# An eight-headed cross-attention rebuilt: context prepared two stages earlier, queries made per tile, scores over 64 inputs in float32, softmax turned in float32

## The reference, cut to what matters

```python
def _L1_xattn_ref(x, context, Wq, Wk, Wv, Wo, bo):      # H = 8, D = 64
    q = (x @ Wq).reshape(B, Nq, H, D)
    k = (context @ Wk).reshape(B, Nkv, H, D)
    v = (context @ Wv).reshape(B, Nkv, H, D)
    sim = jnp.einsum('bihd,bjhd->bhij', q, k) * SCALE   # D ** -0.5
    attn = jax.nn.softmax(sim, axis=-1)
    out = jnp.einsum('bhij,bjhd->bihd', attn, v).reshape(B, Nq, H * D)
    return out @ Wo + bo
...
x = x + L0_attn(layernorm(x));  x = x + L0_xattn(layernorm(x), ctx)   # one head of 256
x = x + L0_ffn(layernorm(x));   x = x + L1_attn(layernorm(x))
x = x + L1_xattn(layernorm(x), ctx);  x = x + L1_ffn(layernorm(x))    # signed weights
```

## Time and profile before

| | us |
|---|---|
| median of 3 runs | 1231.96 (1227.54 to 1237.32) |
| the profiled execution, its own time | 1229.34 |
| its span, first to last instruction | 1227.6 |
| mean granted TensorE clock | 0.894 |
| stage `cross_attention` L = 0 (preparation 283.2 to 334.3, loop to 415) | 132 |
| stage `cross_attention` L = 1, preparation (833.8 to 888.8) | 55.0 |
| stage `cross_attention` L = 1, loop and tail (888.8 to 1038.6) | 149.8 |
| stage `signed_ffn` (from 1039.5) | 188 |

### The profile page before, as it was taken

One profiled execution on the slowest core, in us unless ns is written; L12 is line 12 of the kernel. 1 busy time (PEld: TensorE's weight loads), 2 busy tenths in 40 slices (PEclk: granted clock), 3 DMA queues, 4 the chain that ended last, 5 costly groups with the idle time before them and its releaser, 6 DMA issues. The chain is left out here.

```text
span 1227.6 us, 21445 instructions
## 1 busy us (share of the span) xinstructions
PE 1001.8 (82%) x8092; PEld 580.7 (47%) x8092; DVE 848.9 (69%) x1735; ACT 654.3 (53%) x1106; POOL 337.1 (27%) x409
## 2 busy tenths in 40 slices
PE   2678788881668589998789989975779997899998
PEld 1333333330235345555456666751347775345554
DVE  8859777945567589886788888964678884544322
ACT  5789688982334455532444444433768885433320
POOL 1235645522144100000465555751110000000000
PEclk9889899995555799999999999985579999899999
DMA  2000000004000200000300000004000000000001
GB/s 86 1 1 1 1 1 1 1 1 149 0 1 1 87 1 1 1 1 3 139 1 2 2 2 1 2 2 128 1 2 0 1 1 1 1 1 18 1 18 35
DMA packets 17150, 21.35 MB, mean 17 GB/s; under 512 B 4626, under 2 KB 14496, under 8 KB 16676
## 3 DMA queue, kind: packets, MB, share of 16 engines
q1 hardware_dynamic: 14948, 18.02, 4.5%
q10 hardware_dynamic: 2112, 2.10, 0.5%
HBM read 18.02 MB, written 2.10 MB: 16 GB/s over the span
## 5 line engine op out<-in xcount | busy, mean ns | idle before, releaser
L618 PE MATMUL t_sc<-t_qk 32*128 32x512 f32 (+3 forms) x768 | 118.5, 577 | 41.5 <-ACT t_pT L508 16.2
L508 ACT ACTIVATE t_pT<-t_sc 128x1536 f32<-128x1536 f32 x96 | 136.6, 1452 | 26.9 <-PE t_sc L618 26.1
L2584 PE MATMUL f_psh<-f_h,fs_w 128*128 128x512 f16 x512 | 114.4, 379 | 1.5 <-DVE f_h L2497 1.5
L2497 DVE SCALAR_TENSOR_TENSOR f_h<-f_psh,f_h 128x512 f16<-128x512 f32 x64 | 43.8, 690 | 100.7 <-ACT f_h L2539 100.6
L618 PEld LDWEIGHTS t_sc<-t_qk 32*128 32x128 f32 x768 | 53.8, 206 | 106.7 <-ACT t_pT L508 62.1
L222 POOL TENSOR_SCALAR_AFFINE_SELECT t_pT<-t_pT 128x512 f32<-128x512 f32 x64 | 70.9, 1129 | 120.0 <-ACT t_pT L508 119.5
L2539 ACT ACTIVATE f_h<-f_psh 128x512 f16<-128x512 f32 x64 | 38.2, 597 | 107.3 <-PE f_psh L2584 107.3
L1992 POOL TENSOR_SCALAR_AFFINE_SELECT r_att<-r_att 128x1024 f16<-128x1024 f16 x64 | 73.4, 1170 | 41.0 <-DVE r_att L2031 41.0
L1239 PE MATMUL c_pso<-c_VO,c_pT 128*128 128x256 f16 x576 | 74.5, 287 | 11.7 <-DVE x L1046 6.3
L638 PE MATMUL t_ot<-t_pT,t_v 128*17 128x512 f32 (+3 forms) x768 | 75.2, 520 | 9.5 <-issue 8.9
L2584 PEld LDWEIGHTS f_psh<-f_h,fs_w 128*128 128x128 f16 x512 | 49.8, 98 | 59.0 <-issue 2.0
(11 more groups left out here) (434 smaller groups left out, 2277.2 us busy)
## 6 DMA issues: line engine op xcount, KB each, us to landing
x<-in_x ACTq DMA_DIRECT2D x4, 512.0 KB, 5.9
out_x<-x SPq DMA_DIRECT2D x4, 512.0 KB, 2.9
r_rcos<-in_ret_cos SPq DMA_DIRECT2D x1, 1280.0 KB, 8.2
r_rsin<-in_ret_sin SPq DMA_DIRECT2D x1, 1280.0 KB, 10.7
gw_raw<-in_gateT SPq DMA_DIRECT2D x1, 1024.0 KB, 6.9
gw_raw<-in_upT SPq DMA_DIRECT2D x1, 1024.0 KB, 8.9
gw_raw<-in_downT SPq DMA_DIRECT2D x1, 1024.0 KB, 10.9
fs_k<-in_L_ffn_k SPq DMA_DIRECT2D x1, 1024.0 KB, 11.9
```

The source lines that it names most:

```text
L508: a.activation(pT[:, at:at + 3, :].rearrange("p a s -> p (a s)"), sc[n % 2][:], ACT.Exp, scale=CURVE * CURVE / math.sqrt(2 * DH)).then_inc ...
L618: last = t.matmul(sc[n % 2][:, 512 * k + at:512 * k + at + w], qk[r, g % 2, 1, P * i:P * i + P], qk[r, g % 2, 0, q0:q0 + w], start=(part = ...
L2584: last = mm(psh[:, i % BANKS, :], l, r, start=(k == 0), stop=(k == len(todo) - 1))
```

## The change

- A new class `Keys` makes the context of the eight-headed attention inside `cross_attention` (L = 0): K in float32, V folded with Wo into VO (ten slots a sequence, the bias in a slot of its own through `pick`), and the split query weights `wq16` (turned on TensorE). A is gone. Its 20 trains share two banks and are hung behind the steps of the one-headed preparation by the table `AFTER`; the experts' splits (`Lent`) are moved to later steps. It borrows the room of buffers that the retention uses later (`Ahead`). Its DMAs stand in SP's queue before those of the experts' weights, the first two before the one-headed Wk.
- The wait for the LayerNorm's vectors (`s_wk`) is moved from before the centring of the context to after its normalisation factor.
- The fifth stage is a new function `headed_attention`: no preparation; the square roots come in four spans of tiles; ScalarE normalises; per tile two turns of x in float32, 24 products of 128 columns for the query, 8 scores over 64 inputs and 154 columns in float32 (even heads in rows 0 to 63, odd ones in 64 to 127), maxima already negated, 8 exponentials, two weightings (128 keys on VectorE, the rest on GpSimd), 10 turns in float32, a split at the evacuation (high on ScalarE, low on VectorE), 30 products of 256 columns, the addition.
- `Signs` is spread over the steps of that loop, its largest part on GpSimd.

```diff
+class Keys:
+    STEPS = ([("k", c) for c in range(4)] + [("wq", c) for c in range(2)] + [("v", c) for c in range(4)] +
+             [("vo", (b, h)) for b in range(B) for h in (0, 1, 4, 5)] + [("vr", (b, 0)) for b in range(B)])
+    AFTER = {"var": (0, 1, 2, 3), ("k", 0): (4,), ("k", 1): (5,), ("v", 0): (6,), ("v", 1): (7,), ("qb", 0): (8,), ("c", 0): (9, 10),
+             ("A", (0, 0)): (11, 12), ("A", (0, 1)): (13,), ("VO", (0, 0)): (14, 15), ("VO", (1, 0)): (16, 17),
+             ("VR", (0, 0)): (18,), ("VR", (1, 0)): (19,)}
...
+    def on_tensor(self, t_, event):
+        for i in self.AFTER.get(event, ()):
+            kind, c = self.STEPS[i]
+            ps = self.ps[:, i % 2, :]
+            wait(t_, self.used, i - 1)
...
             if L == 0:
                 v.wait_ge(s_ctx, CTX_IN)
-                v.wait_ge(s_wk, WK_IN)
-
+                keys.on_vector(v, "begin")
                 v.wait_ge(prod, 1)
...
+                v.wait_ge(s_wk, WK_IN)
                 for c, r in ((0, P), (1, CK - P)):
...
+def headed_attention(nc, x, ins, keys, signs):
+    SPANS = ((0, 2), (2, 6), (6, 10), (10, NT))
+    BANKS = ((0, 2, 4), (1, 3, 5), (6, 7))
+    ORDER = (0, 1, 6, 3, 2, 5, 4, 7)
+    GROUPS = ((0, 0, 4), (1, 4, 8), (0, 8, 10))
+        psx, psq, pss, pst, pso = ps("psx", [P, 512]), ps("psq", [P, 512]), ps("pss", [P, 3, 512]), ps("pst", [P, 2, 512]), ps("pso", [P, 512])
+        STEPS = range(-3, NT + 4)
...
+        @block.vector
+            def x_low(t):
+                    v.wait_ge(x_high, t + 1)
+                    v.tensor_tensor(xT[:, t % 2, 2:4, :], psx[:, 0:D]..., xT[:, t % 2, 0:2, :], ALU.subtract).then_inc(x_split, 1)
+            def weigh(t):
+                    v.wait_ge(exp_done, 3 * (t + 1))
+                    wait(v, rest_weighed, t - 1)
+                    v.reciprocal(tot[:, q, 1, :], tot[:, q, 0, :]).then_inc(total_ready, 1)
+                    v.wait_ge(total_ready, t + 1)
+                    wait(v, p_turned, 3 * (t - 1))
+                    v.tensor_tensor(pn[:, q, 0:NH, :], pt[:, q, :, 0:P], ..., ALU.mult).then_inc(main_weighed, 1)
+            def add(t):
+                    v.wait_ge(out_ready, t + 1)
+                    v.scalar_tensor_tensor(x[:, t, :], pso[:, 0:D], 1.0 / XSCALE, x[:, t, :], ALU.mult, ALU.add).then_inc(x_done, 1)
+            for s in STEPS:
+                p_low(s - 2, 0)
+                p_low(s - 2, 1)
+                maxima(s)
+                p_low(s - 2, 2)
+                x_low(s + 2)
+                weigh(s - 1)
+                add(s - 3)
...
+        @block.scalar
+            for s in STEPS:
+                high_p(s - 2, 0)
+                high_p(s - 2, 1)
+                high_p(s - 2, 2)
+                if s >= -1:
+                    normalise(s + 3)
+                exps(s, 0)
+                copy_q(s + 1)
+                exps(s, 1)
+                exps(s, 2)
+                high_x(s + 2)
+                signs.on_scalar(a, s)
...
+        @block.tensor
+            def turn_p(t, j):
+                    if j == 0:
+                        t_.wait_ge(main_weighed, t + 1)
+                        t_.wait_ge(rest_weighed, t + 1)
+                        wait(t_, p_split, 3 * t)
+                    if j == 1:
+                        wait(t_, p_split, 3 * (t - 1) + 2 if t else 0)
+                    if j == 2:
+                        t_.wait_ge(p_split, 3 * t + 1)
+                    for k in range(a, b):
+                        last = t_.transpose(pst[:, bank, P * (k - a):P * (k - a) + P], pn[:, t % 2, k, :], ident[:])
+            def output(t):
+                    t_.wait_ge(p_split, 3 * (t + 1))
+                    wait(t_, x_done, t)
+                    todo = [(pT[:, q, pa, k, :], keys.VO[:, pw, b, k, :]) for k in range(SLOTS) for pa, pw in three]
+            for s in STEPS:
+                score(s)
+                turn_p(s - 2, 2)
+                project(s + 1)
+                turn_x(s + 2)
+                output(s - 2)
+                turn_p(s - 1, 0)
+                turn_p(s - 1, 1)
...
+            if s in (1, 5): statistics(2 + s // 5), spread(2 + s // 5)
```

More of the change, by code:

```diff
@@ L698, in cross_attention @@
+def cross_attention(nc, x, ins, lent, keys, ahead):
+    L, NH, E = 0, 1, 256
     HD = E // NH
@@ L875, in _ @@
             g.wait_ge(s_c, 7)
-            if lent:
-                lent.constants(g, own)
+            keys.constants(g, own)
+            lent.constants(g, own)
             for c in range(EC):
@@ L890, in _ @@
                 last.then_inc(padded, 1)
+            g.wait_ge(padded, EC)
+            keys.pad(g, own)
             def step(s, k):
@@ L1107, in body @@
                 copy_p(s - 1, (k + 1) % 2)
[L1109 to L1115, removed]
+            a.wait_ge(s_ctx, CTX_IN)
+            keys.on_scalar(a, "begin")
+            a.wait_ge(spread, 1)
+            a.activation(half[:], cs, ACT.Sqrt).then_inc(scaled, 1)
+            keys.on_scalar(a, "rooted")
+            keys.on_scalar(a, "var")
+            a.wait_ge(c_normed, 1)
             for n, (src, parts, gain) in enumerate(INPUTS):
@@ L1122, in _ @@
                 a.mul(parts[:, 0], src, gain).then_inc(in_high, 1)
-            for i in PARTED:
-                kind, c = steps[i]
+            for i, (kind, c) in enumerate(steps):
+                if i not in PARTED:
+                    if kind in ("qb", "c"):
+                        keys.on_scalar(a, (kind, c))
+                        lent.on_scalar(a, (kind, c))
+                    continue
                 if kind in "kv":
@@ L2352, in __init__ @@
         self.s, self.sign, self.sign2 = sb("s", [P, 3]), sb("sign", [P, 6]), sb("sign2", [P, 2])
-        self.landed, self.own = [sem(f"landed{j}") for j in range(4)], sem("own")
+        self.landed, self.own, self.differed = [sem(f"landed{j}") for j in range(4)], sem("own"), sem("differed")
         self.scales_ready, self.expanded = sem("scales_ready"), [sem(f"expanded{j}") for j in range(3)]
@@ L2380, in on_vector @@
-        if event == ("v", 3):
-            own.base = 6
-            k0, w0 = self.k[0], self.w[0]
-            v.wait_ge(self.landed[0], 16)
-            L(v.tensor_tensor(w0[:], k0[:, 0:2, :], k0[:, 2:4, :], ALU.subtract))
-            v.tensor_scalar(w0[:], w0[:], sign[:, 0:1], None, ALU.mult).then_inc(self.expanded[0], 1)
-    def on_scalar(self, a, event):
-        piece = {("A", (h, 1)): h // 2 for h in (0, 2, 4, 6)}.get(event)
-        if piece is not None:
+        v.wait_ge(self.landed[3], 3 * 16)
@@ L2627, in program @@
         table_attention(nc, x, ins)
-        with ExitStack() as held:
-            ahead = Ahead(nc, held, held.enter_context(Signals(nc)), x)
-            with ExitStack() as outer:
-                lent = Lent(nc, outer, outer.enter_context(Signals(nc)))
-                cross_attention(nc, x, ins, 0, lent)
-                experts(nc, x, ins, lent, ahead)
-            retention(nc, x, ins, ahead)
-        with ExitStack() as outer:
-            signs = Signs(nc, outer, outer.enter_context(Signals(nc)))
-            cross_attention(nc, x, ins, 1, signs)
-            signed_ffn(nc, x, ins, out, signs)
+        with ExitStack() as known:
+            keys = Keys(nc, known, known.enter_context(Signals(nc)))
+            with ExitStack() as held:
+                ahead = Ahead(nc, held, held.enter_context(Signals(nc)), x)
+                with ExitStack() as outer:
+                    lent = Lent(nc, outer, outer.enter_context(Signals(nc)))
+                    cross_attention(nc, x, ins, lent, keys, ahead)
+                    experts(nc, x, ins, lent, ahead)
+                retention(nc, x, ins, ahead)
+            with ExitStack() as outer:
+                signs = Signs(nc, outer, outer.enter_context(Signals(nc)))
+                headed_attention(nc, x, ins, keys, signs)
+                signed_ffn(nc, x, ins, out, signs)
 def laid_out(a):
```

479 lines of the change are left out of this document (422 added, 57 removed).

## The result

The changed kernel takes 1278.24 us (median of 4 runs, 1274.19 to 1281.58), the kernel before 1230.26 us beside it (4 runs): a ratio of 1.038, 95% interval 1.032 to 1.044. It is slower by 3.8%. The profiled execution of after took 1276.84 us, with a span of 1275.1 and a mean granted clock of 0.882; the span of before was 1227.6.

The account below looks back on a forecast made before the run. The old eight-headed loop was taken as bound by TensorE's columns, the new one by a ring of queue waits. 1229.3 + 10 (keys) - 204.8 (old stage) + 241 (new loop) = 1275.5, forecast 1277 us; own range 1258 to 1302, 8 in 10 1240 to 1302.

Parts of the forecast that it names:

- The keys, +10: One-headed preparation (51.1 us before): taking in the keys' trains adds 10 us, with -2 and +18 as ends.
- the four K trains fall where VectorE normalises the context, which hides them: One-headed preparation: four K trains of 1.8 us each are hidden; without that cover they would cost 7.
- The ring, 13.1 us at the full clock: Eight-headed loop: queue orders close a circle; ScalarE 6.5, VectorE 2.1, TensorE 3.7, hand-overs 0.8 sum to 13.1 us a tile.
- The clock, 1.7 us a tile: Eight-headed loop: TensorE's idle gaps lower the clock, slowing outputs by 0 to 3.2 us; middle 1.7 for twelve steady tiles.
- The 7 us for a start at the low clock: Start of the eight-headed stage: 7 us more because it begins at the low clock.
- the timetable: Eight-headed stage, queues laid out in time: first output after 32 us, distances mostly 13.1, one 14.6; 214 us at full clock.
- (e): Rival, eight-headed loop: ring terms all at their shortest, 11.8 us a tile, total 1235, no change; chance 0.05.
- (b): Rival, eight-headed loop: the ring stands but the clock holds, total 1251, or 1240 with shorter hand-overs; chance 0.16.
- The scores off the path: Eight-headed loop: scores, query products and maxima lie beside ScalarE's part; non-overlapping score halves, 1.0 us more, would lie off path.
- (a): Rival, eight-headed loop: the ring is cut at the output bank, 9.5 us a tile, stage 173, total 1207; chance 0.09.
- (c): Rival, eight-headed loop: the clock stays low throughout, 17.7 us a tile, stage 302, total 1336; chance 0.05.
- (d): Rival, one-headed preparation: the keys do not fit, +25 there in place of +10, total 1291; chance 0.05.

Follow-up runs that it names:

- experiment 7: Changed kernel with ScalarE's copies of Wv's high parts moved behind the first key chunk: 1278.97 us; the same edit with experiment 3's order: 1192.24 us.
- experiment 4: Changed kernel, order kept, with 38 filler products of 256 columns on TensorE ahead of each output's wait: 1264.70 us, 1.025 of the kernel before.
- experiment 3: Changed kernel with add(s - 3) at the head of VectorE's step and x_low(s + 2) at its end: 1190.66 us, 0.966 of the kernel before.
- experiment 1: Changed kernel with only add(s - 3) moved from the end to the head of VectorE's step: 1216.78 us, 0.989 of the kernel before.
- experiment 8: Changed kernel with all twenty key trains run behind the last train of the one-headed preparation, not between its trains: 1286.44 us, 1.044 of the kernel before.

## Why the prediction came out right

**The keys, +10.** +11.5, with some luck. VectorE was set free as forecast (the centring starts 2.7 us after the context's first product, at 289.75, where it was 6.0; the earlier trace rows has the wait that is gone). The step "the four K trains fall where VectorE normalises the context, which hides them" failed in part: ScalarE's queue held a transfer's wait ahead of their copies, 4 us. So the split of the context starts 19.75 us after the first product, 0.8 later than before and not 3 earlier; with that wait out of the way, in experiment 7, it is 15.65, the 3 us forecast. Behind it, 13 more were forecast and 10.1 came (39.0 us for 28.9). There the clock rose, from about 326 us on, which I had only allowed for ("may lift the clock"). The two errors, nearly 4 us one way and 3 the other, about cancel.

**The ring, 13.1 us at the full clock.** 12.91 in experiment 4. The terms, from the tile shown: ScalarE 6.5 forecast, 6.7 with its hand-over to VectorE; third copy 2.1 us after the first for 1.9; VectorE 2.1 and two hand-overs for 2.27 measured up to the output's start; turns 0.43 and a hand-over for 0.64. The one longer distance of the timetable, 14.6, doesn't show: in experiment 4 ten in a row are 12.91 or 12.92. The sum held because it was added along the queues and not by busy time, which has the tile at 7.5 to 7.7 us: experiment 3 shows that number to be reachable, in another order.

**The clock, 1.7 us a tile.** 14.87 less 12.91 is 1.96; the output trains took 4.70 to 6.36 us for 3.44 at the full clock. The middle between "holds" and "low throughout" was a choice that no row of before settled, and that it came within 0.3 us is luck. The 7 us for a start at the low clock were too many: the first output started 30.5 us after the stage's start, where the timetable with them has 35.7. The fifteen distances took 204.0 for 201.5 (the first ten 148.7 for 149.5, the last five 55.3 for 52.0), and the end 4.8 for 3.8. So 241 against 239.3, with errors of -5.2, +2.5 and +1.0. In the text of the prediction a count is wrong, its sum is not: sixteen outputs have fifteen distances, so nine of 13.1 and not ten stand beside the one of 14.6, and 214 is the sum with nine. Three smaller sums are off too: as much idle between the keys' trains as now would give +22 by its own numbers and not +18, (e) and half of (b) are 0.13 and not 0.12, and the range's ends lie 1 or 2 us further out than 1258 to 1302. None of them moves the forecast.

**The scores off the path.** This held for the most part only. Eight heads' scores took 1.37 us for 1.05 and the 24 query products 1.50 for 1.35, beside ScalarE's copies, normalisation and exponentials. GpSimd's weighting took 1.57 (0.6 forecast, 1.8 at most) and was over before the output starts, while the turns that need it stand behind the output. The query products and GpSimd's part don't show in the distance. The scores do, a little: by an estimate from the tile shown, VectorE's first subtraction had ended at about 974.4 (it began at 973.69, and one of the two takes some 0.7), and the two turns that it releases start at 974.70, straight behind the scores, so these hold up ScalarE's third copy by about 0.3 us. That is the 2.1 for 1.9 above, and it means that the 1.0 us more for scores whose halves don't overlap would have lain on the path and not off it.

**The rivals.** (a), 1207 us if the bank's release left the ring, is experiment 1: 9.68 us a tile for 9.5, a stage of 175.3 us for 173, 1216.78 in all; of the 10 us between the totals 7 lie in the stretch between the one-headed loop and the stage (506.6 us for 499.6), which varies in any order. The price of the mechanism was right, and what spoke against it, the order as written, decided. (b), the clock holds, is experiment 4 in its steady part; by itself it does not hold in this order. (c) and (e) did not occur, (d) neither: the keys took less than half of 25.

**The rule of the skill.** The Trainium skill (Perfetto Trace Analysis, Optimizing Tensor Performance) wants groups of products to rotate through banks. The wait ahead of each output, 5.36 us, is for the one bank, and so the trace agrees with the rule in this order of the queue; in the kernel before, TensorE was busy for the whole of a tile with one bank. But the bank was only the place where the wait showed: with one bank still, experiments 1 and 3 take it away. A second bank was not tried.

## What to carry to other kernels

Before a stage is priced by its busiest engine, walk once around the queues: from the last operation of an engine's step to what waits for it, to what stands behind that in its queue, and on until you are back. If the walk closes within one step, its sum is a lower bound of the step, and here it was the step. An operation that releases something (a bank, a buffer) belongs at the head of its engine's step, and one that waits for another engine's last operation belongs at the end; here that is worth 88 us of 1278 with no work changed. And a gap that such a circle leaves on TensorE cost twice here, once as a gap and once as the slower products behind it.

## What the runs showed of the hardware

**The clock does not follow the gap alone.** In the changed kernel ten gaps ahead of the outputs are alike to 0.01 us (5.35 to 5.36), yet the trains behind them take 5.12, 6.34, 5.29, 4.75, 6.14, 5.19, 4.70, 6.12, 5.17 and 6.36 us, close to a pattern of three. With x_low last, gaps of 1.93 us are followed by trains of 3.44 or 5.10 us, while in experiment 1 gaps of 1.8 us ahead of the turns leave fifteen of sixteen outputs at 3.45. In experiment 8 the clock falls near 337.7 us within the keys' trains, though TensorE was busy for 10.9 of the 12 us from 325 to 337 and no idle time listed from there to the fall is longer than 0.83 us; it is 0.50 for some ten us in which TensorE is busy for 95% (338 to 347.5 us), and then 1.00 again. Which gap makes which train slow stays open; that filling the gaps makes all of them fast is shown (experiment 4).

**VectorE and GpSimd take turns.** GpSimd's weighting of 208 elements is shown with 1.57 us in all 16 tiles, starting 0.05 us after VectorE's weighting of 1.22 us. The added operation took 1.21 us in all 16 tiles ahead of x_low, where GpSimd stands idle (in three tiles from 939 to 970 us), and 1.56 in all 16 behind the weighting, while GpSimd is at work; GpSimd's piece for the signs (L2892), begun beside it, took 2.16 us instead of 1.19:

```profile
948.56 1.57 POOL L1527 TENSOR_TENSOR c_pn<-c_pt,c_tot 128x208 f32<-128x208 f32 x1 [8.19 <-DVE c_tot L1586]
950.11 2.16 POOL L2892 TENSOR_SCALAR fs_w<-fs_k,fs_sign 128x1024 f16<-128x1024 uint8 x1
```

If each holds what both need for its whole length, GpSimd starts at 949.7, when the weighting ends, and VectorE's next gets through some 0.35 us later, which is the 1.56, by my estimate. The Trainium skill (SBUF — State Buffer, SBUF: two separate sides) states just that: the pair of ports that the two engines share is an exclusive lock, held for the whole instruction, by VectorE's operations that read two inputs in SBUF as well, against a GpSimd operation that reads SBUF. The trace agrees with it.
